# Shifted planes written out to DRAM, first stacks loaded as one transfer each, second stacks filled by ScalarE copies and two late loads

## The chip, the cores and the metric

The kernel runs on one core of one Trainium2 chip. The metric is the device time of one execution in microseconds (us). Engines: TensorE (PE in the profile; PEld is its weight load), VectorE (DVE), ScalarE (ACT), GpSimd (POOL) and SyncE (SP), which here only issues transfers. ACT also issues transfers of its own.

## The reference, cut to what matters

```python
def _gn(v, G=32): ...                  # group norm, 2 channels a group
def _L0_conv_ref(x, weight, scale):    # 3x3 convolution of signs
    y = conv(sign(x), sign(weight), padding=1)
    return y * scale[None, :, None, None]
def _L1_conv_ref(x, ...):              # involution, 7x7, 16 groups of 4 channels
    r = relu(batchnorm(w_r @ x + b_r))             # 64 -> 16 channels
    ker = w_s @ r + b_s                            # 16 -> 49*16: a 7x7 kernel for each pixel and group
    for ki in range(7):
        for kj in range(7):
            out += xp[:, :, :, ki:ki+H, kj:kj+W] * ker[:, :, ki*7+kj][:, :, None]
    return out
x = x + _L0_conv_ref(_gn(x), ...)      # x is (32, 64, 56, 56), float32
x = x + _L1_conv_ref(_gn(x), ...)
```

## The kernel before

Two images make a pair; 16 pairs go through one after the other, and nearly all time is the involution. The kernel swaps its order: for each patch of the normalised image it first multiplies by the weights of every reduced channel (PE), multiplies that by r (DVE, `prod`), and adds up (POOL `folded`, then PE `sums`).

**Strips and units.** The image of a pair is cut into 7 strips of 8 columns (`E = 7`). A strip has 8 units (`GP = 8`), each for two of the 16 groups, so a pair has 56 units, numbered n = 0 to 55. A unit is 8 matmuls of `taps` (L567) into a bank of two halves, one DVE product (L788) and one POOL addition (L361). Three PSUM banks go round among units, convolution chunks (`conv`), transposes (`t`), the reduction (`red`) and outputs, in the order that `turns` lists; a PE step waits until the bank's user of three turns ago has been read.

**Stacks.** The matmuls of strip e read patches from two tiles in SBUF: `X1` ("patches", three buffers, the first stack) and `X2` ("patches2", two buffers, the second stack). A stack's 128 partitions are 8 planes of 16 partitions; a plane is an image part (0 the fp16 value, 1 its fp16 rest) shifted by some rows. On before:
- `first_stack(e)` on SP: eight transfers from DRAM, one a plane (16 partitions, 4 pieces of 3584 B each; L283). It waits until strip e-3 has been read by the matmuls, and that the parts of its pair are in DRAM.
- `second_stack(e)` on SP: two transfers (planes that the first stack hasn't; L291). The other five planes stand in partitions 0 to 95 of the first stack, and ACT copies them there (`copy_high`, L428, four copies of 96 partitions a strip) in the strip before the one that needs them.
- `taps` of a strip's first unit waits for the first stack, for the second stack's transfers, and for the copies.

`PLANES` is the table of part, shift, first partition and partition step of each plane.

**How the parts come to DRAM.** In pair p, while its strips run, pair p+1 is prepared: sums of the image on DVE (n = 0 to 3), `sign` on ACT (n = 5), convolution chunks (n = 11, 12, 14, 17), `root` and `normalize` on ACT (n = 18, 21), four transposes (n = 28, 30, 34, 36), each followed by `high` on ACT (L400) and `low` on DVE (L779), which write the two fp16 parts into a tile with two slots, then `parts_out` on SP (two transfers of 256 KB for each of the four; L266). `high` of transpose k waits until `parts_out` of k-2 has landed. At n = 37 and 38 `red` and `relu` (ACT, L408) make r, and `spread` on SP copies it in 16 transfers of 49 KB (L301) from the tile "blocks" to the tile "relu" that the products read. The first product of the next pair waits for it.

**Results.** `gather(e)` on ACT (L416) takes a strip's sums from PSUM and writes them to DRAM, `rows(e)` on ACT reads them back rearranged, `arrange` on ACT (L450) writes them into "blocks" (the same memory as r before the spread), at n = 46 for strips 0 to 3 and at n = 13 of the next pair for strips 4 to 6; PE transposes them back and DVE adds them to the image, which `store` on SP writes out.

**What sets the order.** Each engine's program is written out by hand, and so is the SP queue: in strip s of pair p it issues the second stack of e+1, the first stack of e+2, `parts_out` 0 and 1 in strip 3, and 2, 3 and the spread in strip 4; the image of pair p+2 is loaded in strip 3. SP works through that list in order, so an entry that waits holds all behind it.

```python
COPY_AT = {0: 0, 1: 1, 4: 2, 5: 3}     # unit of the strip: which of the four copies of the next strip
SUMS_B, BIAS, SUMS_A, ROWS_AT = 3, 6, 7, 7 # units of gather, bias matmuls, first half of sums, rows
```

## Time and profile before

| | before |
|---|---|
| three runs | 1944.62 us median (1939.9 to 1957.48) |
| the profiled execution's own time | 1947.81 us |
| its span, first to last instruction | 1945.9 us |
| granted TensorE clock, mean | 0.922 of full speed |
| PE, DVE, ACT, POOL busy | 83%, 71%, 54%, 52% |
| DMA: moved, mean rate | 410.67 MB, 211 GB/s |
| transfers issued for stacks | 1120 of 224 KB |

The page gives one execution. Times of an instruction are ns or us; "idle before, releaser" is how long its engine had stood still before it and what ended that. In a timeline, "x8" is eight instructions merged in one row. SPq and ACTq are rows of the transfer-issuing sequencers: their time is that of issuing, not of the transfer. Strips are told apart in the timeline by SP's rows: `first_stack(e+2)` starts as soon as strip e-1 has been read.

### The profile page before, as it was taken

The page shows a single profiled execution, that of the slowest core. Times are in us where ns is not written, and L with a number is a line of the kernel's source. Part 1 is how long each engine was busy: PE and PEld are TensorE (multiplying, and loading weights), DVE is VectorE, ACT ScalarE, POOL GpSimd, SP SyncE. Part 2 cuts the span into 40 slices and gives each one's busy share as a digit, 9 for nine tenths or more (in the row PEclk, how much of TensorE's full clock was granted, in tenths as well). Part 3 has the DMA queues.
Part 4 walks back from the last instruction along what each step waited for, and adds up shares of the span by engine and source line. Part 5 has one row for each costly group of instructions (what it writes and reads, how often), then busy time and mean ns, then how long its engine had stood idle before and what let it go on. Part 6 is the DMA issues. An engine that isn't in the chain of part 4 may idle for free.

```text
span 1945.9 us, 38822 instructions
## 1 busy us (share of the span) xinstructions
PE 1615.7 (83%) x15072; PEld 730.2 (38%) x15072; DVE 1377.2 (71%) x1699; ACT 1054.9 (54%) x758; POOL 1016.5 (52%) x904
## 2 busy tenths in 40 slices
PE   3488897979889798897978889798897978889785
PEld 2233443434344343343434344343343433344342
DVE  6476786858678686786858678676786858678574
ACT  2355566555656455565545656454565545656443
POOL 1145565454655555465554655555565454655573
PEclk8699998999999899998989999898998999999897
DMA  3669899797998979799797998979799797988992
GB/s 108 166 168 242 187 261 217 189 245 175 253 211 229 231 192 245 183 260 208 204 229 187 257 199 238 226 188 241 188 254 215 197 236 181 254 206 227 208 248 85
DMA packets 211592, 410.67 MB, mean 211 GB/s; under 512 B 83822, under 2 KB 131231, under 8 KB 207263
## 3 DMA queue, kind: packets, MB, share of 16 engines
q1 hardware_dynamic: 136144, 356.79, 73.1%
q10 hardware_dynamic: 75264, 51.39, 10.2%
q8 instruction: 119, 1.95, 0.5%
q14 instruction: 65, 0.53, 0.1%
HBM read 310.30 MB, written 84.93 MB: 203 GB/s over the span
## 4 chain that ended last, share of the span: by engine, by line
POOL 49%; issue 42%; PE 2%; SPq 2%; DVE 2%; DMA 2%; ACT 1%; POOLq 1%; ACTq 0%; DVEq 0%
POOL folded L361 49%; SPq L301 1%; PE ybank L508 1%; POOLq L360 1%; SPq L283 0%; DMA patches<-parts_dram 0%; PE ybank L567 0%; DMA xs<-x_dram 0%; DVE rowsums L730 0%; DVE prod L788 0%; DMA parts_dram<-parts 0%; PE ybank L537 0%; PE ybank L548 0%; ACT patches L428 0%; ACT sgn L381 0%
## 5 line engine op out<-in xcount | busy, mean ns | idle before, releaser
L361 POOL TENSOR_TENSOR folded<-prod 128x448 f32<-128x448 f32 x896 | 1010.8, 1141 | 911.7 <-DVE prod L788 910.9
L788 DVE TENSOR_TENSOR prod<-ybank,relu 128x896 f32<-128x896 f32 x896 | 960.9, 1088 | 405.7 <-PE ybank L567 336.3
L567 PE MATMUL ybank<-patches,wspan 128*64 128x448 f16 x7168 | 863.2, 383 | 240.8 <-ACT patches L428 106.0
L428 ACT ACTIVATE patches<-patches 96x1792 f16<-96x1792 f16 x448 | 736.6, 1689 | 554.7 <-DMA patches<-parts_dram 273.7
L567 PEld LDWEIGHTS ybank<-patches,wspan 128*64 128x64 f16 x7168 | 400.2, 117 | 757.2 <-issue 421.7
L508 PE MATMUL ybank<-sgn,convw 128*128 128x448 bf16 x1008 | 206.4, 358 | 21.4 <-ACT sgn L381 17.0
L585 PE MATMUL obank<-folded,esum 128*32 128x448 f32 x1792 | 214.8, 551 | 1.5 <-POOL folded L361 1.5
L578 PE MATMUL obank<-patches,wbias 128*32 128x448 f16 x3584 | 197.1, 363 | 0.0
L508 PEld LDWEIGHTS ybank<-sgn,convw 128*128 128x128 bf16 x1008 | 93.7, 98 | 135.3 <-issue 31.5
L578 PEld LDWEIGHTS obank<-patches,wbias 128*32 128x32 f16 x3584 | 87.1, 98 | 103.8 <-issue 50.9
L746 DVE SCALAR_TENSOR_TENSOR xs<-ybank,scale,xs 128x896 f32<-128x896 f32 x64 | 66.0, 1032 | 74.9 <-PE ybank L508 74.8
L779 DVE TENSOR_TENSOR parts<-ybank,parts 128x1024 f16<-128x1024 f32 x64 | 78.3, 1223 | 38.3 <-ACT parts L400 38.0
L400 ACT ACTIVATE parts<-ybank 128x1024 f16<-128x1024 f32 x64 | 65.7, 1027 | 63.1 <-PE ybank L537 59.4
L599 PE MATMUL ybank<-back,blocks 128*128 128x128 f32 (+1 forms) x448 | 61.1, 281 | 43.9 <-DVE prod L788 36.0
L416 ACT ACTIVATE osb<-obank,alpha 128x448 f32<-128x448 f32 x112 | 69.6, 621 | 40.0 <-PE obank L585 39.6
L450 ACT ACTIVATE blocks<-rows 128x1792 f32<-128x1792 f32 (+1 forms) x32 | 54.1, 1691 | 46.3 <-DMA relu<-blocks 33.4
L599 PEld LDWEIGHTS ybank<-back,blocks 128*128 128x128 f32 (+1 forms) x448 | 47.4, 150 | 75.7 <-DVE prod L788 49.5
L750 DVE BATCH_NORM_STATS2 bn<-xs 128x6 f32<-128x448 f32 x112 | 70.3, 627 | 3.9
L537 PE MATMUL ybank<-ident,xn 128*128 128x128 f32 x512 | 71.0, 284 | 1.0 <-DVE parts L779 0.2
L800 DVE TENSOR_TENSOR xs<-ybank,xs 128x1024 f32<-128x1024 f32 (+1 forms) x64 | 61.8, 966 | 12.1 <-PE ybank L599 12.0
L392 ACT ACTIVATE xn<-xs,small 128x1568 f32<-128x1568 f32 x32 | 58.9, 1897 | 17.1 <-DVE small L772 17.0
L730 DVE TENSOR_REDUCE rowsums<-xs 128x14 f32<-128x784 f32 x64 | 61.1, 958 | 9.5 <-DMA xs<-x_dram 9.5
(90 smaller groups left out, 378.0 us busy)
## 6 DMA issues: line engine op xcount, KB each, us to landing
patches<-parts_dram SPq DMA_DIRECT2D x1120, 224.0 KB, 7.1
parts_dram<-parts SPq DMA_DIRECT2D x128, 256.0 KB, 5.4
xs<-x_dram SPq DMA_DIRECT2D x16, 1568.0 KB, 9.7
sums_dram<-osb ACTq DMA_DIRECT2D x112, 224.0 KB, 6.2
rows<-sums_dram ACTq DMA_DIRECT2D x112, 224.0 KB, 6.7
out_dram<-xs SPq DMA_DIRECT2D x16, 1568.0 KB, 5.9
relu<-blocks SPq DMA_DIRECT2D x256, 49.0 KB
patches<-gb_dram SPq DMA_DIRECT2D x1, 784.0 KB
```

Of the source, the lines that this page charges most:

```text
L361: pool.tensor_tensor(folded[:, u % 8, :], prod[:, u % 2, 0, :], prod[:, u % 2, 1, :], ALU.add).then_inc(fold_done, 1)
L416: act.activation(osb[:], Obank[e % 2][:, 0:N], ACT.Copy, scale=alpha[:]).then_inc(o_read, 1)
L428: act.activation(X2[0:COPIED_ROWS, e % 2, at], X1[0:COPIED_ROWS, e % 3, at], ACT.Copy).then_inc(copied, 1)
L508: mm = pe.matmul(bank("conv", p, k)[:, i, 0:CW], convw[:, tap, :], sgn[:, CR * row + dh:CR * row + dh + CR, dw:dw + W], start=(tap == 0), ...
L537: mm = pe.transpose(bank("t", p, k)[:, y, 128 * h:128 * h + 128], xn[:, COLS * cy:COLS * cy + COLS], ident[:])
L567: mm = pe.matmul(bank("unit", p, n)[64 * t:64 * t + 64, h, 0:N], wspan[:, stack, g, h, :], of_group(e, stack, g), start=(stack == 0), stop ...
L578: pe.matmul(Obank[e % 2][32 * t:32 * t + 32, 0:N], wbias[:, stack, g, :], of_group(e, stack, g), start=(stack == 0 and i == 0), stop=False)
L585: mm = pe.matmul(Obank[e % 2][32 * (gp // 2):32 * (gp // 2) + 32, 0:N], esum[:, 16 - 16 * (gp % 2):48 - 16 * (gp % 2)], folded[:, 4 * half ...
L599: mm = pe.transpose(bank("out", p, k)[:, i, rows * n:rows * (n + 1)], V[0:rows, by].rearrange("m b g c -> m (b g c)"), back[0:rows, group, ...
L750: link(dve.bn_stats(bn[:, row, :], at[:, i, :]))
L779: dve.tensor_tensor(at(1), bank("t", p, k)[:], at(0), ALU.subtract).then_inc(low_done, 1)
L788: dve.tensor_tensor(prod[:, u % 2].rearrange("m h (n c) -> m h n c", c=GC), bank("unit", p, n)[:, :, 0:N].rearrange("m h (n c) -> m h n c" ...
```

## The change

`parts_out` now writes all ten planes out, each already shifted, into two DRAM tensors: `D0` holds the eight planes of the first stack side by side, `D1` the two planes that only the second stack has. That is ten transfers for k = 0 and six for each of k = 1, 2, 3 (28 a pair, where there were 8 of 256 KB), of rows of 1024, 768 or 512 B; a source that goes to several planes is read once for each of them in the same transfer. `first_stack` is one transfer of 128 partitions by 4 pieces of 3584 B. Partition 8r+q now holds row r of plane q. The second stack's order is such that six of its eight planes (one of them unused) stand where the first stack has them, so ACT copies all 128 partitions, and planes 3 and 7 are then overwritten by two transfers that ACT itself issues after the four copies. The copies move to units 0 to 3, `rows(e-2)` to unit 3 (it was `rows(e-1)` at 7), `gather` to 4. The spread and the image load move to strip 5, behind the first stack's transfer. r gets a tile of its own (`rsum`), so `relu` and `arrange` lose three waits; `arrange` of the second group moves from n = 13 to 15.

```diff
-PLANES = (((0, 0, 32, 4), (0, 4, 0, 2), (0, 1, 33, 4), (1, 0, 96, 2),
-           (0, 2, 34, 4), (1, 1, 1, 2), (0, 3, 35, 4), (1, 2, 97, 2)), ...
+PLANES = (((0, 0), (0, 2), (0, 4), (1, 1), (0, 1), (0, 3), (1, 0), (1, 2)),
+          ((0, 0), (0, 2), (0, 4), (1, 3), (0, 1), (0, 3), None, (1, 4)))
+LOADED = (3, 7)
-FIRSTLOAD, SECONDLOAD = 16 * 8, 16 * 2
+FIRSTLOAD, SECONDLOAD = 16, 16 * 2
-DWRITE = 16 * 2
+DWRITE = (16 * 10, 16 * 6)
-ARRANGE1_AT, ARRANGE0_AT = 13, 46
-SUMS_B, BIAS, SUMS_A, ROWS_AT = 3, 6, 7, 7
+ARRANGE1_AT, ARRANGE0_AT = 15, 46
+SUMS_B, ROWS_AT, GATHER, BIAS, SUMS_A = 3, 3, 4, 6, 7
-COPY_AT = {0: 0, 1: 1, 4: 2, 5: 3}
+COPY_AT = {0: 0, 1: 1, 2: 2, 3: 3}
...
-        rsum = V[:].rearrange("p y b g c -> p (y b g c)")[:, 0:PX * 2 * HW // POS].rearrange("p (x n) -> p x n", x=PX)
+        rsum = sb("rsum", [128, PX, 2 * HW // POS])
...
 def parts_out(p, k):
-                for l in range(2):
-                    sp.dma_start(D[p % 2, l].rearrange(...)[:, :, k, :], Ev[:, l, k % 2]).then_inc(d_written[k], 16)
+                def run(dram, planes, q, l, y, shift, many):
+                    src = Ev[:, l, k % 2, y]
+                    if k == 0:
+                        for i in range(many):
+                            cut = BLOCK * (shift + i)
+                            sp.dma_start(dram[b, :, q + i, 0:4 * BLOCK - cut], src[:, cut:]).then_inc(d_written[k], 16)
+                        return
+                    dst = bass.AP(..., ap=[[planes * RUN, 128], [RUN - BLOCK, many], [1, 4 * BLOCK]])
+                    sp.dma_start(dst, src.unsqueeze(1).broadcast_to((128, many, 4 * BLOCK))).then_inc(d_written[k], 16)
+                run(D0, Q, 0, 0, 0, 0, 3)
+                run(D0, Q, 4, 0, 1, 0, 2)
+                run(D0, Q, 6, 1, 0, 0, 2)
+                run(D0, Q, 3, 1, 1, 0, 1)
+                run(D1, 2, 0, 1, 1, 1, 1)
+                run(D1, 2, 1, 1, 0, 2, 1)
 def first_stack(e):
-                for l, a, row, step in PLANES[0]:
-                    sp.dma_start(X1[row:row + 15 * step + 1:step, e % 3, :], plane(e, l, a))...
+                sp.dma_start(X1[:, e % 3, :].rearrange("p (j n) -> p j n", j=JX), stack(D0, e)).then_inc(first_in[e % 3], 16)
-            def second_stack(e):    # on SP, waits y_ready
...
                     e = E * p + s
-                    if e + 1 < EALL:
-                        second_stack(e + 1)
...
                         if s == 4:
                             parts_out(p + 1, 2)
                             parts_out(p + 1, 3)
+                        if s == 5:
                             spread(p + 1)
-                    if s == 3 and p + 2 < pairs:
+                    if s == 5 and p + 2 < pairs:
...
-                act.activation(X2[0:COPIED_ROWS, e % 2, at], X1[0:COPIED_ROWS, e % 3, at], ACT.Copy).then_inc(copied, 1)
+                act.activation(X2[:, e % 2, at], X1[:, e % 3, at], ACT.Copy).then_inc(copied, 1)
+            def second_stack(e):    # on ACT
+                act.wait_ge(copied, JX * (e + 1))
+                ...
+                for i, q in enumerate(LOADED):
+                    src = bass.AP(tensor=D1.tensor, ..., ap=[[2 * RUN, 16], [8 * RUN, JX], [1, JY * 128]])
+                    act.dma_start(X2[q:128:Q, e % 2, :]..., src).then_inc(second_in[e % 2], 16)
...
 def arrange(group):
-                act.wait_ge(r_spread, SPREAD * min(p + 1 + (group % 2 == 0), pairs))
...
+                    if n % GP in COPY_AT and e + 1 < EALL:
+                        copy(e + 1, COPY_AT[n % GP])
+                        if COPY_AT[n % GP] == JX - 1:
+                            second_stack(e + 1)
+                    if n % GP == ROWS_AT and e > 1:
+                        rows(e - 2)
+                    if n % GP == GATHER and e > 0:
+                        gather(e - 1)
```

The SP queue in strips 3 to 6 of a pair ("patches" is both stacks' tile, "parts_dram" the DRAM tensor of the parts). Before:

```order
L266 DMA parts_dram<-parts 256x1x512 x4
L254 DMA xs<-x_dram 128x3136
L291 DMA patches<-parts_dram 16x4x1792 x2
L283 DMA patches<-parts_dram 16x4x1792 x8
L266 DMA parts_dram<-parts 256x1x512 x4
L301 DMA relu<-blocks 16x1x784 x16
L291 DMA patches<-parts_dram 16x4x1792 x2
L283 DMA patches<-parts_dram 16x4x1792 x8
```

Now, from the last rows of `parts_out(p+1, 1)` on ("planes_dram" stands for D0 and D1):

```order
L281 DMA planes_dram<-parts 128x512 x3
L302 DMA patches<-planes_dram 128x4x1792
L281 DMA planes_dram<-parts 128x3x512
L281 DMA planes_dram<-parts 128x2x512 x2
L281 DMA planes_dram<-parts 128x512 x3
L281 DMA planes_dram<-parts 128x3x512
L281 DMA planes_dram<-parts 128x2x512 x2
L281 DMA planes_dram<-parts 128x512 x3
L302 DMA patches<-planes_dram 128x4x1792
L311 DMA relu<-rsum 16x1x784 x16
L257 DMA xs<-x_dram 128x3136
L302 DMA patches<-planes_dram 128x4x1792 x4
```

The second stack's rows are gone from SP, ten stack entries a strip have become one, the spread stands behind a first stack and not ahead of one, and the image load stands behind the spread.

ACT in strip 4 (L400 and L408 are `high` and `relu`, L416 with L420 `gather`, L441 `rows`, L428 the copies). Before:

```order
L428 ACTIVATE patches<-patches 96x1792 x2
L400 ACTIVATE parts<-ybank 128x1024
L416 ACTIVATE osb<-obank,alpha 128x448
L420 DMA sums_dram<-osb 128x448
L400 ACTIVATE parts<-ybank 128x1024
L428 ACTIVATE patches<-patches 96x1792
L408 ACTIVATE blocks<-ybank,red_bias,red_scale 128x2x392
L428 ACTIVATE patches<-patches 96x1792
L408 ACTIVATE blocks<-ybank,red_bias,red_scale 128x2x392
L441 DMA rows<-sums_dram 32x16x112
```

Now, the same strip (L434 the copies, L445 the second stack's transfers, L408 `high`, L414 `relu`, L422 and L426 `gather`, L457 `rows`):

```order
L434 ACTIVATE patches<-patches 128x1792 x2
L408 ACTIVATE parts<-ybank 128x1024
L434 ACTIVATE patches<-patches 128x1792 x2
L445 DMA patches<-planes_dram 16x4x1792 x2
L457 DMA rows<-sums_dram 32x16x112
L408 ACTIVATE parts<-ybank 128x1024
L422 ACTIVATE osb<-obank,alpha 128x448
L426 DMA sums_dram<-osb 128x448
L414 ACTIVATE rsum<-ybank,red_bias,red_scale 128x2x392 x2
```

All four copies and the two transfers now stand ahead of the strip's second `high`; both `relu` come after them in one piece.

## Rows read from the trace of the kernel before

**Rows 1.** The page's second part: busy tenths of 40 slices, DMA share, GB/s.

```profile
DMA  3669899797998979799797998979799797988992
DMA packets 211592, 410.67 MB, mean 211 GB/s; under 512 B 83822, under 2 KB 131231, under 8 KB 207263
q1 hardware_dynamic: 136144, 356.79, 73.1%
q10 hardware_dynamic: 75264, 51.39, 10.2%
```

**Rows 2.** Waits: engine, line, what it waited for; us in total, times, longest.

```profile
PE ybank L567 <- ACT patches L428: 106.0, 29, 20.7
PE ybank L567 <- DMA patches<-parts_dram: 103.9, 15, 8.1
ACT patches L428 <- DMA patches<-parts_dram: 273.7, 43, 13.0
SPq L266 <- DVE parts L779: 134.9, 43, 44.7
```

**Rows 3.** Timeline of PE, strip 5 to the next pair's strip 0: start, length.

```profile
981.92 0.95 PE L567 MATMUL ybank<-patches,wspan 128*64 128x448 f16 x8
992.71 0.96 PE L585 MATMUL obank<-folded,esum 128*32 128x448 f32 x8
1001.50 4.60 PE L567 MATMUL ybank<-patches,wspan 128*64 128x448 f16 x24 [7.82 <-DMA patches<-parts_dram]
1014.63 0.96 PE L585 MATMUL obank<-folded,esum 128*32 128x448 f32 x8
1019.49 2.83 PE L567 MATMUL ybank<-patches,wspan 128*64 128x448 f16 x14 [3.90 <-ACT patches L428]
```

**Rows 4.** Timeline of the transfers that SP issues, the same stretch and the next spread.

```profile
963.54 5.73 SPq L266 DMA_DIRECT2D parts_dram<-parts  x4
971.51 5.02 SPq L283 DMA_DIRECT2D patches<-parts_dram  x8
976.63 4.42 SPq L266 DMA_DIRECT2D parts_dram<-parts  x4
983.16 13.50 SPq L301 DMA_DIRECT2D relu<-blocks  x16
996.76 1.26 SPq L291 DMA_DIRECT2D patches<-parts_dram  x2
998.25 5.01 SPq L283 DMA_DIRECT2D patches<-parts_dram  x8
1100.75 12.07 SPq L301 DMA_DIRECT2D relu<-blocks  x16
```

**Rows 5.** Busy time by stretch: bounds; PE, PEld, DVE, ACT, POOL; PEclk, DMA share, GB/s.

```profile
939.00:946.00 7.00, 6.12 (x51) 2.84 (x49) 6.47 (x12) 0.87 (x1) 4.50 (x4) 1.00 1.03 244
951.50:953.50 2.00, 2.00 (x38) 0.85 (x36) 1.86 (x7) 1.12 (x1) 0.06 (x1) 1.00 0.96 401
56.00:65.00 9.00, 3.42 (x32) 0.40 (x32) 2.55 (x3) 4.14 (x4) 0.00 (x0) 0.74 0.69 227
```

**Rows 6.** Timeline of ACT in strips 4 to 6.

```profile
971.67 1.00 ACT L400 ACTIVATE parts<-ybank 128x1024 f16<-128x1024 f32 x1
975.30 1.03 ACT L400 ACTIVATE parts<-ybank 128x1024 f16<-128x1024 f32 x1 [1.24 <-PE ybank L537]
993.08 3.28 ACT L428 ACTIVATE patches<-patches 96x1792 f16<-96x1792 f16 x2 [0.46 <-PE ybank L567]
998.79 1.70 ACT L450 ACTIVATE blocks<-rows 128x1792 f32<-128x1792 f32 x1 [2.43 <-DMA relu<-blocks]
```

**Rows 7.** By line, issue to landing: L283, L291, then L441 (`rows`).

```profile
DMA to landing us min/median/max: 3.0/7.4/15.0
DMA to landing us min/median/max: 3.3/5.5/12.9
DMA to landing us min/median/max: 2.8/6.7/16.7
```

**Rows 8.** Timeline at the start: the first parts and the first product.

```profile
54.53 8.41 SPq L266 DMA_DIRECT2D parts_dram<-parts  x8
85.28 1.09 DVE L788 TENSOR_TENSOR prod<-ybank,relu 128x896 f32<-128x896 f32 x1 [23.56 <-DMA relu<-blocks]
```

More of the change, by code:

```diff
@@ L398, in high @@
                     before = 4 * p + k - 2
-                    act.wait_ge(d_written[before % 4], DWRITE * (before // 4 + 1))
+                    act.wait_ge(d_written[before % 4], DWRITE[before % 4 > 0] * (before // 4 + 1))
                 act.activation(Ev[:, 0, k % 2], bank("t", p, k)[:], ACT.Copy).then_inc(high_done, 1)
@@ L427, in copy_high @@
                 at = slice(COPY * j, COPY * (j + 1))
-                act.activation(X2[0:COPIED_ROWS, e % 2, at], X1[0:COPIED_ROWS, e % 3, at],
-                               ACT.Copy).then_inc(copied, 1)
+                act.activation(X2[:, e % 2, at], X1[:, e % 3, at], ACT.Copy).then_inc(copied, 1)
+            def second_stack(e):
+                act.wait_ge(copied, JX * (e + 1))
+                if e >= 2:
+                    act.wait_ge(second_in[e % 2], SECONDLOAD * (e // 2))
+                p = e // E
+                for i, q in enumerate(LOADED):
+                    src = bass.AP(tensor=D1.tensor, offset=(2 * (128 * (p % 2) + 4 * JX * (e % E)) + i) * RUN,
+                                  ap=[[2 * RUN, 16], [8 * RUN, JX], [1, JY * 128]])
+                    act.dma_start(X2[q:128:Q, e % 2, :].rearrange("p (j n) -> p j n", j=JX), src).then_inc(second_in[e % 2], 16)
             def rows(e):
@@ L473, in _ @@
                         relu(p + 1, RED_AT[n])
-                    if n % GP == SUMS_B and e > 0:
+                    if n % GP in COPY_AT and e + 1 < EALL:
[5 more added lines that the diff above has]
+                    if n % GP == GATHER and e > 0:
                         gather(e - 1)
-                    if n % GP in COPY_AT and e + 1 < EALL:
-                        copy_high(e + 1, COPY_AT[n % GP])
-                    if n % GP == ROWS_AT and e > 0:
-                        rows(e - 1)
                     if more and n == SIGN_AT:
@@ L489, in _ @@
                         arrange(2 * p)
+            rows(EALL - 2)
             gather(EALL - 1)
@@ L850, in constants @@
             for stack in range(2):
-                for part, a, row, step in PLANES[stack]:
+                for q, plane in enumerate(PLANES[stack]):
+                    if plane is None:
+                        continue
+                    part, a = plane
                     sel = stack if part or stack == 0 else 2
@@ L856, in constants @@
                         if 0 <= ky < K and 0 <= kx < K:
-                            c[ky * K + kx, C_SEL + 384 * pos + 128 * sel + row + step * r] = 1
+                            c[ky * K + kx, C_SEL + 384 * pos + 128 * sel + Q * r + q] = 1
     for m in range(128):
```

38 lines of the change are left out of this document (15 added, 23 removed), and 3 rows, old and new, of the table PLANES.

## The prediction

> **What bounds the kernel now.** I read the waits first. Summed over the run, PE stands still before a unit's matmuls for 106.0 us because of ACT's copies and for 103.9 us because of a stack's transfer [rows 2]. The longest single one, 20.7 us, is the start. (106.0 + 103.9 - 20.7)/16 = 11.8 us a pair.
>
> The timeline says where. Strip 5 ends its matmuls at 993.67 us, and strip 6 begins at 1001.50 after 7.82 us of waiting for a transfer; strip 6 ends at 1015.59, and the next pair's strip 0 begins at 1019.49 after 3.90 us of waiting for the copies [rows 3]. So 11.7 us of this pair are two waits, and together with the sum above I take these two as the whole of it. The pair lasts 117.6 us, from one spread to the next [rows 4].
>
> SP's queue explains both. It issues 16 spread transfers in 13.50 us, from 983.16; only then, at 996.76, come the second stack of strip 6 and, at 998.25, the first stack of strip 0 [rows 4]. The matmuls of strip 6 wait for the first, the copies for strip 0 wait for the second.
>
> The transfers themselves are the next bound: queues 1 and 10 together take 83.3% of the 16 DMA engines' span, and most slices stand at 7 to 9 tenths [rows 1]. What to see in the rates: a stretch in which only stacks are loaded is fully busy at 244 GB/s, one in which the image is stored is fully busy at 401 GB/s [rows 5]. A busy DMA engine moves stack planes at 0.6 of the rate it reaches elsewhere. ACT's copies wait 273.7 us for first stacks [rows 2]. POOL, which the page's chain shows most, has half its time idle and follows DVE.
>
> **The change part by part**, for one pair.
>
> *SP's queue.* Stack issues fall from 70 to 7. Eight first-stack issues take 5.02 us and two second-stack ones 1.26 [rows 4], so 44 us a pair go. The spread moves behind the first stack of the next pair's strip 0, and no second stack stands behind it any more. Both waits of [rows 3] lose their cause: minus 11.7 us. `parts_out` goes from 8 issues to 28. Four take 4.42 us with a wait in them, eight at the start 8.41 with waits [rows 4, 8]; without the waits about 0.6 us each; 28 cost 17 us, and SP has the 44.
>
> *The second stack's chain.* What was parallel is now serial: all four copies, then two issues on ACT, then the transfer. Two copies take 3.28 us [rows 6], four 6.6; 128 partitions by 1792 elements should cost ACT what 96 did, since its time went by elements. Two issues add about 0.6. The landing: the same two transfers took 3.3 us at least and 5.5 in the middle [rows 7]. Chain from the end of strip e-1 to the second stack of e+1: 6.6 + 0.6 + 5.5 = 12.7 us, 10.5 at best.
> - Strip 6: the last matmuls of strip 4 end at 982.87, and PE is free for strip 6 at 993.67, 10.8 us later [rows 3]. New wait: 12.7 - 10.8 = 1.9 (0 at best).
> - Strip 0: `arrange` at n = 46 now waits for `rows` of strip 3, which ACT only issues behind strip 6's chain: 982.9 + 6.6 + 0.6 = 990.1, landing 2.8 to 6.7 later [rows 7], arranged after 1.7 [rows 6]: 994.6 to 998.5. Then the chain: 1007.3 to 1011.2. PE would be free for strip 0 at 1015.59 - 7.82 + 1.9 = 1009.7. Wait 0 to 1.5; I take 1.5, because the landings under load have been nearer to the median.
> - Strip 1: its first stack stands behind the spread and behind the 1568 KB of the image, but strip 0 is long. 0.5.
> - Strips 3 and 4: 12 to 14 us for the chain, with `normalize`, `root` and `high` between the copies. 0.5 each.
>
> *ACT's order in strips 3 and 4.* `high` at n = 28 now stands behind all four copies, the second stack's issue and `rows`, not behind two copies: two copies later (3.3 us), of which half is covered by PE's two spare banks: 1.5. `high` at n = 36, which ran at 975.30 [rows 6], likewise: two copies and two issues come first, 1.6. DVE's `low` and all products stand behind it. 3.1 together (1.5 to 5). `high` of k = 2 and 3 also waits for `parts_out` of k = 0 and 1, now 10 and 6 issues (6 and 4 us) where two stood. The first `high` of strip 4 ran at 971.67, 8.1 us after SP began on the first parts at 963.54 [rows 4, 6], so this just fits; at 1 us an issue it would not.
>
> *DMA load.* A pair wrote 8 x 256 KB = 2.1 MB. Now k = 0 writes 128 x (4 x 1024 + 4 x 768 + 2 x 512) B and each other k 128 x 10 x 1024 B, 5.0 MB in all: 2.9 MB more. Such writes ran at 227 GB/s at a share of 0.69, so 329 at full share [rows 5]: 8.8 us more. Against that, 12.8 of the 16 MB of stacks come in transfers of 128 partitions. If these run at the 401 GB/s of the other 128-partition transfer instead of 244 [rows 5], they take 32 us and not 53. Sum: 0.833 x 117 = 97 us, minus 20.6, plus 8.8: 85 us of 114. If they stay at 244: 106 of 114. I take the first, half-heartedly, and charge 0.4 for collisions. The Trainium skill, "SBUF — State Buffer", section "Door 1: The DMA port swizzle", states that partitions reach 16 ports by groups of four, so that 16 partitions at a step of 2, as six of the ten planes have here, reach only 8 of them; "DMA: Bandwidth & Descriptors", section "The descriptor swizzle", gives each engine of a 128-partition transfer one port. The 244 against 401 of the trace agrees. By that rule the stacks run at the faster rate and the two late planes, at a step of 8, at the slower.
>
> *Own tile for r.* `arrange` waited 2.43 us for the spread at 998.79 [rows 6]; that wait goes, and I booked the one that takes its place above. The moved image load waits for nothing that PE needs until the sums of the next pair.
>
> *Ends.* Start: 28 issues instead of 8, from 54.53 on [rows 8], delay the first stack by 6 to 10 us; then copies and second stack in a chain, where now the first product waits for the spread until 85.28 [rows 8]. Plus 9. In the last pair no spread stands in the way before, yet strips wait for stacks; minus 6.
>
> Sum for a pair: 11.7 - (1.9 + 1.5 + 0.5 + 1.0 + 3.1 + 0.4) = 11.7 - 8.4 = 3.3 us gained. 15 x 3.3 = 50; 50 + 6 - 9 = 47. The profiled execution took 1947.81 us, so 1901; it lies 3 above the median of the runs. I say 1900.
>
> **The rivals.**
> 1. *Nothing moves.* The stacks keep 244 GB/s, the queues are busy for 106 of 114 us, and landings on ACT's queue rise by about 1 us. Three to four strips' waits follow, and the 3.3 us are gone: 1935 to 1965, say 1950. For it: the trace has no 128-partition load out of this DRAM layout, so 401 may have to do with the image's layout and not with the partitions. Against it: the surplus is in packets that the queues take well.
> 2. *The chain is the new bound, slower.* Place: copies to second stack, on ACT. If it lands after 7.4 us, as half of the first-stack transfers took or more, and `rows` nearly (6.7) [rows 7], each of strips 6, 0, 1, 3, 4 waits 1.9 us longer: 9 us more a pair, 5.7 worse than before: 1945 + 86 + 3 = 2034. It decides from a landing of about 6.4 us on. For it: the first stack of e+2 is issued at the same moment as the copies begin, and the same engines move both. The Trainium skill, "DMA: Bandwidth & Descriptors", section "Queues, rings and completion order", says an engine goes round between its queues packet by packet, which would double the second stack's moving time while a first stack is under way. Against it: a first stack at 401 GB/s is through in 4.6 us, before the copies end.
> 3. *All hidden.* Landings of 3.3 us, so waits of 0 at strips 6, 0, 1, 3, 4, and 1.5 for ACT's order: 11.7 - 1.9 = 9.8 a pair, 147 + 6 - 9: 1801.
>
> **How the numbers follow.** Chances: forecast 0.43, nothing moves 0.22, slower 0.22, all hidden 0.13. The forecast's own range is 1870 to 1930: chain 1 us shorter or longer changes three or four waits, about 2 us a pair, 30 us. The range of 8 in 10 reaches from 1830 (towards the third rival) to 1990 (halfway into the second). About 1% is what a measurement of this kernel can tell from no change. Faster by over 1% (below 1925): nearly all of the forecast, 0.13 of the third and a little of the first, 0.54. Within 1% (to 1964): 0.22. Slower: 0.24.
>
> **What would show it.** PE's waits of 7.82 and 3.90 us at strips 6 and 0 become 1 to 2 us, and the one at strip 6 names the second stack's transfer on ACT's queue. The first stack lands about 5 to 7 us after its issue, and a stretch with stacks alone shows over 350 GB/s; if it shows 244, rival 1 stands. The second stack's landing, by its line, is 4.5 to 6; over 6.4, rival 2. `high` in strip 4 comes 1.5 us later relative to its transpose; if it instead waits for the parts' transfers, my 0.6 us an issue is wrong, and with it the forecast. The first product comes at 92 to 97 us.

## The result and the profile after

The changed kernel takes 2025.87 us (median of four; 2016.25 to 2028.85) against 1944.18 us (also of four), a ratio of 1.040 with a 95% interval of 1.034 to 1.046: 82 us slower, where 45 us faster was forecast. The profiled execution spans 2021.2 us, 75 us more than the one of before.

The page after, second and third part, against [rows 1]:

```profile
DMA  3738678585875958668585885848768586775873
DMA packets 253316, 456.75 MB, mean 226 GB/s; under 512 B 76398, under 2 KB 172959, under 8 KB 248991
q1 hardware_dynamic: 159952, 351.51, 50.2%
q10 hardware_dynamic: 93184, 102.79, 19.5%
```

The two queues moved 46 MB more in less of the engines' time, 69.7% of the span and not 83.3%. So the transfers did get cheaper, and the time went elsewhere. The waits after, against [rows 2]:

```profile
ACT blocks L465 <- DMA rows<-sums_dram: 204.0, 32, 11.8
PE ybank L586 <- DMA patches<-planes_dram: 146.6, 36, 31.4
DVE parts L798 <- ACT parts L408: 107.4, 52, 5.5
ACT patches L434 <- DMA patches<-planes_dram: 82.7, 16, 13.3
```

ACT waits much less for first stacks (82.7 us, before 273.7) and PE not at all for ACT's copies, but PE waits more for a stack's transfer (it is the second stack), and two waits have grown: `arrange` for the rows (204.0, before 12.9), and `low` on DVE for `high` on ACT (107.4, before 38.0). PE in turn waits for `arrange`, which cost it 7.9 us before:

```profile
PE ybank L618 <- ACT blocks L465: 53.2, 15, 7.7
```

The timeline of PE in strip 6 and at the next strip 0, against [rows 3]:

```profile
1041.88 0.96 PE L604 MATMUL obank<-folded,esum 128*32 128x448 f32 x8
1043.70 2.46 PE L586 MATMUL ybank<-patches,wspan 128*64 128x448 f16 x24 [0.86 <-DMA patches<-planes_dram]
1051.64 1.94 PE L618 MATMUL ybank<-back,blocks 128*128 128x128 f32 x8 [5.48 <-ACT blocks L465]
1062.18 0.96 PE L604 MATMUL obank<-folded,esum 128*32 128x448 f32 x8
1067.05 3.20 PE L586 MATMUL ybank<-patches,wspan 128*64 128x448 f16 x16 [3.91 <-DMA patches<-planes_dram]
```

Strip 6 starts after 0.86 us of waiting, where it was 7.82. But after its third unit PE stands 5.48 us for `arrange`, and strip 0 still starts 3.91 us late. This pair is one of the better ones at strip 6: in the mean over pairs 1 to 14 PE waits 3.33 us at the start of strip 6 and 3.69 at strip 0, both for the second stack's transfers. On the kernel before it was 6.96 and 3.84. ACT in the same stretch, against [rows 6]:

```profile
1032.17 6.45 ACT L434 ACTIVATE patches<-patches 128x1792 f16<-128x1792 f16 x4
1038.65 1.21 ACTq L445 DMA_DIRECT2D patches<-planes_dram  x2
1039.98 0.52 ACTq L457 DMA_DIRECT2D rows<-sums_dram  x1
1040.60 0.63 ACT L422 ACTIVATE osb<-obank,alpha 128x448 f32<-128x448 f32 x1 [1.98 <-issue]
1049.80 1.70 ACT L465 ACTIVATE blocks<-rows 128x1792 f32<-128x1792 f32 x1 [8.57 <-DMA rows<-sums_dram]
1051.40 6.44 ACT L434 ACTIVATE patches<-patches 128x1792 f16<-128x1792 f16 x4
1057.87 1.19 ACTq L445 DMA_DIRECT2D patches<-planes_dram  x2
```

`rows` goes out behind four copies and two issues, lands 9.8 us later, and `arrange` and the copies for strip 0 stand behind it.

The second stack's transfers land after 4.2 us in the median of the whole run, but not where PE waits for them. From the issue of the second transfer to its landing, strips 1 to 4 take 4.0 to 4.4 us in the median (pairs 1 to 14), strip 6 takes 7.7 and strip 0 7.4. Two strips 6 show the difference, first pair 9, then pair 10 (issues of SP and ACT, then the landing of ACT's two):

```profile
1285.47 0.37 SPq L302 DMA_DIRECT2D patches<-planes_dram  x1
1285.80 1.19 ACTq L445 DMA_DIRECT2D patches<-planes_dram  x2
DMA to landing us min/median/max: 7.5/8.1/8.7
```

```profile
1406.74 1.19 ACTq L445 DMA_DIRECT2D patches<-planes_dram  x2
1407.87 0.37 SPq L302 DMA_DIRECT2D patches<-planes_dram  x1
DMA to landing us min/median/max: 3.3/3.7/4.1
```

In pair 9 a first stack is issued just ahead, and PE waits 5.34 us; in pair 10 it is issued 1.1 us after the first of ACT's two transfers, and PE waits 0.73. In the eight strips 6 of pairs 1 to 14 in which the first stack was issued at most 0.2 us after the second transfer, or before it, that transfer took 7.7 to 8.9 us; in the other six, 4.1 to 5.5. No run varied this by itself.

Length of each strip in us, first product to first product, from the timelines of DVE, mean over pairs 1 to 14 of 0 to 15:

| strip | 0 | 1 | 2 | 3 | 4 | 5 | 6 | pair |
|---|---|---|---|---|---|---|---|---|
| before | 13.9 | 21.4 | 17.3 | 12.8 | 15.9 | 17.7 | 17.5 | 116.5 |
| after | 13.8 | 21.3 | 17.4 | 14.6 | 18.6 | 13.7 | 21.8 | 121.4 |

4.9 us a pair, 73 in 15 pairs; the first product comes at 99.27 us and not at 85.28, 14 more; the last pair, from first to last product, takes 82.9 us and not 90.4, 7.5 less. In sum some 80 us, against 75 in the spans (the table's mean leaves pair 0 out).

### The profile page after: what moved, and what is told of

It is laid out like the page before. It is cut to its first block, busy times and chain, and to the rows that moved or that the text cites. A ratio compares the mean times of both kernels' runs of the same rounds, so it can differ in the third digit from the quotient of the medians.

```text
span 2021.2 us, 38357 instructions
## 1 busy us (share of the span) xinstructions
PE 1634.8 (81%) x15072; PEld 729.0 (36%) x15072; DVE 1378.9 (68%) x1699; ACT 1049.6 (52%) x758; POOL 1013.8 (50%) x904
## 3 DMA queue, kind: packets, MB, share of 16 engines
q1 hardware_dynamic: 159952, 351.51, 50.2%
## 4 chain that ended last, share of the span: by engine, by line
POOL 39%; issue 38%; DMA 7%; ACT 5%; DVE 4%; PE 4%; ACTq 1%; SPq 1%; POOLq 0%; DVEq 0%
POOL folded L369 39%; DMA rows<-sums_dram 4%; ACT patches L434 4%; DMA patches<-planes_dram 2%; DVE prod L807 1%; PE ybank L586 1%; ACTq L445 1%; DMA back<-consts_dram 1%; PE ybank L618 1%; ACT blocks L465 1%; DVE parts L798 1%; PE obank L597 1%; PE ybank L567 1%; ACT parts L408 0%; SPq L281 0%
## 5 line engine op out<-in xcount | busy, mean ns | idle before, releaser
L434 ACT ACTIVATE patches<-patches 128x1792 f16<-128x1792 f16 x448 | 725.2, 1684 | 185.1 <-PE ybank L586 97.3
L586 PEld LDWEIGHTS ybank<-patches,wspan 128*64 128x64 f16 x7168 | 390.3, 115 | 742.1 <-issue 350.8
L527 PE MATMUL ybank<-sgn,convw 128*128 128x448 bf16 x1008 | 205.6, 357 | 22.0 <-ACT sgn L389 17.5
L604 PE MATMUL obank<-folded,esum 128*32 128x448 f32 x1792 | 220.2, 564 | 1.5 <-POOL folded L369 1.5
L597 PE MATMUL obank<-patches,wbias 128*32 128x448 f16 x3584 | 206.2, 376 | 0.0
L422 ACT ACTIVATE osb<-obank,alpha 128x448 f32<-128x448 f32 x112 | 70.8, 632 | 180.1 <-issue 146.4
L465 ACT ACTIVATE blocks<-rows 128x1792 f32<-128x1792 f32 (+1 forms) x32 | 54.3, 1697 | 204.0 <-DMA rows<-sums_dram 204.0
L798 DVE TENSOR_TENSOR parts<-ybank,parts 128x1024 f16<-128x1024 f32 x64 | 78.3, 1223 | 107.7 <-ACT parts L408 107.4
L618 PE MATMUL ybank<-back,blocks 128*128 128x128 f32 (+1 forms) x448 | 67.1, 299 | 90.3 <-ACT blocks L465 53.2
L408 ACT ACTIVATE parts<-ybank 128x1024 f16<-128x1024 f32 x64 | 65.5, 1023 | 133.3 <-issue 56.9
L618 PEld LDWEIGHTS ybank<-back,blocks 128*128 128x128 f32 (+1 forms) x448 | 52.3, 161 | 123.7 <-issue 68.0
L389 ACT ACTIVATE sgn<-xs,small 128x3136 bf16<-128x3136 f32 x16 | 46.6, 2914 | 70.4 <-DVE small L758 67.5
L556 PEld LDWEIGHTS ybank<-ident,xn 128*128 128x128 f32 x512 | 57.7, 146 | 52.2 <-DVE parts L798 36.7
```

Source lines behind the costliest of these rows:

```text
L422: act.activation(osb[:], Obank[e % 2][:, 0:N], ACT.Copy, scale=alpha[:]).then_inc(o_read, 1)
L434: act.activation(X2[:, e % 2, at], X1[:, e % 3, at], ACT.Copy).then_inc(copied, 1)
L465: act.activation(V[0:rows].rearrange("m y b g c -> m g y b c"), U[0:rows].rearrange("m g y (b c) -> m g y b c", b=2), ACT.Copy).then_inc(a ...
L527: mm = pe.matmul(bank("conv", p, k)[:, i, 0:CW], convw[:, tap, :], sgn[:, CR * row + dh:CR * row + dh + CR, dw:dw + W], start=(tap == 0), ...
L556: mm = pe.transpose(bank("t", p, k)[:, y, 128 * h:128 * h + 128], xn[:, COLS * cy:COLS * cy + COLS], ident[:])
L586: mm = pe.matmul(bank("unit", p, n)[64 * t:64 * t + 64, h, 0:N], wspan[:, stack, g, h, :], of_group(e, stack, g), start=(stack == 0), stop ...
```

## The experiments

Eighteen runs, each compared with the kernel before on the same chip. "Changed" is the changed kernel, 2026 us.

### Where the time went, first round

**e1: rows where they were.** Edit to the changed kernel:

```diff
-ARRANGE1_AT, ARRANGE0_AT = 15, 46
-SUMS_B, ROWS_AT, GATHER, BIAS, SUMS_A = 3, 3, 4, 6, 7
+ARRANGE1_AT, ARRANGE0_AT = 13, 46
+SUMS_B, ROWS_AT, GATHER, BIAS, SUMS_A = 3, 7, 4, 6, 7
-                    if n % GP == ROWS_AT and e > 1: rows(e - 2)      # behind copy and second_stack
+                    if n % GP == ROWS_AT and e > 0: rows(e - 1)      # behind gather
```

> The changed kernel with one part undone: rows(e-1) at unit 7 again and not rows(e-2) at unit 3 (arrange of the second group at n = 13 again, which the order needs). Theory A (the result transfers): in strip 6 arrange waits about 9 us for rows that ACT issued too late, PE waits about 5.5 us for it before the outputs at n = 50, and the copies for strip 0 start late behind it. Then 4.6 us of strip 6 and 2 to 3 us at strip 0 go, about 7 us a pair, and the time is 1910 to 1935. Theory B (the chain copies, second stack on ACT is the bound, my second rival): what precedes the chain doesn't matter much, the time stays within 15 us of 2026.

Measured: 2035.42 us (ratio to before 1.048, 1.043 to 1.054), no gain. Strip 6 fell from 21.8 to 18.0 us, as theory A has it, and strips 3 and 5 rose from 14.6 and 13.7 to 16.7 and 16.4: ACT now waits for the sums to reach DRAM before it may issue `rows`, and the next strip's copies stand behind that wait.

```profile
ACT patches L434 <- DMA sums_dram<-osb: 98.3, 31, 9.4
```

The wait moved along ACT's queue. That speaks for B, but it doesn't dismiss A: this edit removes one wait and makes another. e13 moves `rows` without that, and gains.

**e2: the spread's new place alone.** Edit to the kernel before: r in a tile of its own (this makes two of the waits needless, not three as said above), and

```diff
                             parts_out(p + 1, 3)
-                            spread(p + 1)
+                        if s == 5:
+                            spread(p + 1)
```

> The kernel before with r in a tile of its own and the spread issued in strip 5, behind the second and first stack of that strip, nothing else. If the two waits of 7.8 and 3.9 us a pair come from the order of SP's queue, as the prediction's first term says, 8 to 11 us a pair go: 1780 to 1830. If they come from the rate of the stack transfers (244 GB/s, queues 83% busy), the stacks land as late as before and it stays at 1920 to 1945.

Measured: 1949.21 us, ratio 1.004 (1.000 to 1.008). Strip 5 fell from 17.7 to 13.6 us, and strips 6, 0 and 1 rose from 17.5, 13.9 and 21.4 to 19.0, 16.4 and 22.8. The waits:

```profile
ACT patches L427 <- DMA patches<-parts_dram: 401.3, 58, 15.1
PE ybank L565 <- ACT patches L427: 139.4, 34, 19.7
```

The copies' wait for first stacks grew from 273.7 to 401.3 us. With SP's order out of the way, the landing of the first stacks was next in line. Whether it is late by the transfers' slow rate alone, this run doesn't tell, for SP now also stands still before those transfers until the parts have landed:

```profile
SPq L281 <- DMA parts_dram<-parts: 102.2, 32, 6.7
```

The first term of my sum, 11.7 us a pair, is worth nothing by itself.

**e3: the copies' new places alone.** Edit to the kernel before:

```diff
-COPY_AT = {0: 0, 1: 1, 4: 2, 5: 3}
+COPY_AT = {0: 0, 1: 1, 2: 2, 3: 3}
```

> The kernel before with its copies at units 0 to 3 and not 0, 1, 4, 5, nothing else. The strips 3 and 4 of the changed kernel are 1.8 and 2.7 us longer than before. If that is ACT's order (high behind four copies), this costs 3 to 4.5 us a pair: 1990 to 2010. If it is the waits of high for the 28 part transfers, or the issue of transfers on ACT, this costs under 1 us a pair: 1945 to 1960.

Measured: 1991.2 us, 46 more than before (1.027, 1.022 to 1.032): 3.1 us a pair. So ACT's order costs this much with no change to any transfer. But only 1.5 of it stands in strips 3 and 4 (13.4 and 16.8 us); strips 0 and 1 grew by 1.9, and PE's wait for the copies at the start of strip 1 from 0.75 to 2.33.

**e4: no second-stack transfers.** Edit to the changed kernel, which leaves out the second stack's two loaded planes after the first strip:

```diff
-                    act.dma_start(X2[q:128:Q, e % 2, :]..., src).then_inc(second_in[e % 2], 16)
+                    if e == 0:
+                        act.dma_start(X2[q:128:Q, e % 2, :]..., src).then_inc(second_in[e % 2], 16)
```

> The changed kernel without the two second-stack transfers (left out but for the first strip, with the waits for them; so two planes of the second stack hold what the copies left and the output is not the reference's). Theory B (the chain's last link bounds): the gaps of 3.2 us at strip 6 and most of 3.8 us at strip 0 go and ACT saves 1.2 us a strip: 6 us or more a pair, 1920 or below. Theory A (arrange bounds strips 6 and 0): 1 to 3 us a pair, 1980 to 2010.

Measured: 1831.43 us, 194 less than the changed kernel. Theory B. The arrange wait fell with it, and `rows` landed after 3.3 us in the median (6.1 in the changed kernel):

```profile
ACT blocks L466 <- DMA rows<-sums_dram: 79.0, 32, 7.9
PE ybank L588 <- DMA patches<-planes_dram: 32.1, 1, 32.1
```

PE's only wait for a stack's transfer is the start's. A pair takes 109.5 us. So 194 us hang on these 224 transfers, as a wait, as traffic, or as ACT's issue time. Strip 6's arrange wait, theory A, hangs on them too; what it costs alone is for e13.

### Partitions of a transfer, and the chain again

**e5: a second stack that needs no copy first**, with planes written out as in the changed kernel; **e6: the same with the chain put back.** e5 gives the six copied planes partitions 0 to 95 and loads the others into 96 to 127:

```diff
+SHARED = ((0, 0, 0, 6), (0, 2, 1, 6), (0, 4, 2, 6), (0, 1, 3, 6), (0, 3, 4, 6))
+PLANES = (SHARED + ((1, 1, 5, 6), (1, 0, 96, 2), (1, 2, 97, 2)), SHARED + ((1, 3, 96, 2), (1, 4, 97, 2)))
-                sp.dma_start(X1[:, e % 3, :]..., stack(D0, e))
+                sp.dma_start(X1[0:96, e % 3, :]..., stack(D0, e, 6))
+                sp.dma_start(X1[96:128, e % 3, :]..., stack(DL, e, 2))
+            def second_stack(e):      # on SP, ahead of first_stack(e + 1); e6: on ACT, behind the copies
+                sp.dma_start(X2[96:128, e % 2, :]..., stack(D1, e, 2)).then_inc(second_in[e % 2], 16)
```

> The changed kernel with another plane order: the six planes that ACT copies stand in partitions 0 to 95, the two that the second stack loads in 96 to 127, so the second stack's transfer (one of 32 partitions, on SP, issued before the first stack of e+2) needs no copy first. First stack as two transfers (96 and 32 partitions), copies at units 0, 1, 4, 5, rows(e-1) at unit 7, image load in strip 3, spread in strip 5; planes written out as in the changed kernel. Theory C (the serial chain copies, then second stack is what the change lost by; written planes and traffic are affordable): PE's waits at the strips' starts shrink to 2 to 4 us a pair, 111 to 114 us a pair, 1850 to 1900. Rival D (the traffic: 46 MB more written, 51 MB of second stacks): the waits stay, 1980 or more.

> The kernel of e5 with the second stack's transfer on ACT behind the four copies, nothing else. Same bytes, same transfers. Theory C: each strip's chain is back and starts at unit 5: 8 us or more a pair over e5, 2000 to 2050. Rival D: within 20 us of e5.

Measured: e5 2082.01 us, e6 2283.6. e5 came out slower than the changed kernel, but that says nothing of the written planes, for its first stacks had become slow. The third part of the page of e5 has

```profile
q1 hardware_dynamic: 177872, 402.90, 78.9%
```

For 51 MB more on this queue (the second stacks) the time rose from 50.2% of 2021 us to 78.9% of 2083. A first stack in 96 and 32 partitions isn't the first stack in 128. As a test of C, e5 is spoiled; e6 against e5 isn't: the same bytes in the same transfers, and the chain behind copies that end at unit 5, with the issue on ACT in place of SP, costs 202 us.

**e7 and e8: the first stack in eight transfers**, out of the changed kernel's DRAM planes, at a step of 8 partitions or in neighbouring ones:

```diff
-                sp.dma_start(X1[:, e % 3, :]..., stack(D0, e)).then_inc(first_in[e % 3], 16)
+                for q in range(Q):                                     # e7
+                    sp.dma_start(X1[q:128:Q, e % 3, :]..., src).then_inc(first_in[e % 3], 16)
+                for i in range(8):                                     # e8
+                    sp.dma_start(X1[16 * i:16 * i + 16, e % 3, :]..., src).then_inc(first_in[e % 3], 16)
```

> The changed kernel with the first stack as eight transfers of 16 partitions at a step of 8, out of the same DRAM planes. If the stacks' slow rate before (244 GB/s alone) came from few partitions a transfer, which reach few of SBUF's ports, a stretch with stacks alone shows 220 to 260 GB/s again; if it came from the layout in DRAM, over 330.

> The same with 16 neighbouring partitions a transfer. If neighbouring partitions share a port in fours, this is as slow as e7 or slower (under 220 GB/s in a stretch with stacks alone); if the DRAM layout decides, over 330.

Measured, one run each: 2206.08 and 2750.86 us. Stretches with stack loads alone, first the changed kernel, then e7, then e8 (bounds; PE, PEld, DVE, ACT, POOL; PEclk, DMA share, GB/s):

```profile
961.50:965.50 4.00, 3.85 (x40) 2.22 (x40) 3.66 (x4) 4.00 (x4) 3.67 (x4) 1.00 1.02 403
```

```profile
1086.00:1090.00 4.00, 4.00 (x40) 1.93 (x38) 3.45 (x5) 4.00 (x4) 3.68 (x4) 1.00 1.06 226
```

```profile
1182.50:1186.50 4.00, 1.96 (x20) 1.06 (x16) 3.72 (x11) 0.64 (x2) 1.13 (x1) 1.00 1.09 125
```

Same source, same pieces of 3584 B, engines fully busy: 403, 226 and 125 GB/s. The layout in DRAM is the same in all three, so it doesn't decide the rate; which partitions one transfer writes does, and with them which of the same pieces it reads. By the port rule of the Trainium skill ("SBUF — State Buffer", "Door 1: The DMA port swizzle"), a transfer of e7 reaches 8 ports and one of e8 only 4 of 16; the measured ratios, 0.56 and 0.31, agree in order and lie somewhat above 8/16 and 4/16.

### The chain's parts, and attempts to mend it

**e9: the second stack's transfers made tiny.** The rest of the two planes is left out.

```diff
-ap=[[2 * RUN, 16], [8 * RUN, JX], [1, JY * 128]]
+ap=[[2 * RUN, 16], [8 * RUN, JX], [1, 64]]
```

> The changed kernel with its second-stack transfers cut to the first 64 of each 1792 elements (the rest of those two planes is left out); the same two transfers on ACT, behind the same four copies, with the same waits. It lies between e4 (no transfer, no wait: 1831) and the changed kernel (2026). Theory C, the serial wait: even a tiny transfer lands 3.3 us or more after its issue, so most of the 195 us stay, 1940 to 2000. Rival D, the traffic of these 16-partition transfers (174 us of the 16 engines' time) and what it delays: 1835 to 1880.

Measured: 1947.02 us. Against e4 (1831) the waits and issues without bytes cost 116 us; the bytes cost the other 79. These transfers land after 2.6 us in the median, the full ones after 4.2:

```profile
patches<-planes_dram ACTq DMA_DIRECT2D x224, 8.0 KB, 2.6
```

```profile
patches<-planes_dram ACTq DMA_DIRECT2D x224, 224.0 KB, 4.2
```

(e9, then the changed kernel). At strips 6 and 0 the tiny ones, too, took 7.1 and 5.8 us.

The strips show where the two parts fall. All that the bytes cost stands in strip 6, 15.8 us here and 21.8 in the changed kernel. The waits at the starts of strips 6 and 0 differ by 0.9 us a pair; what differs most is PE's wait for `arrange`, 11.1 us in all against 53.2, because the rows landed sooner. Of the other part, 3.9 us a pair stand in strips 3 and 4 (13.1 and 16.5 us in e4, 14.7 and 18.8 here), where PE waits for no stack at all: there `high` comes later on ACT, which in e9 stands idle for 60.5 us in all between issuing transfers and `high`, and never in e4. So the 116 us are the serial wait and ACT's issue time together, and no run parts them.

**e10: SP's old order in the changed kernel.**

```diff
-                        if s == 5:
                             spread(p + 1)
-                    if s == 5 and p + 2 < pairs:
+                    if s == 3 and p + 2 < pairs:
```

> The changed kernel with the spread in strip 4 and the image load in strip 3 again, ahead of first stacks, nothing else. If moving them gained what the prediction's first term says, this loses 5 us or more a pair, 2090 to 2140. If, as in e2, their place is worth little, it stays within 20 us of 2026.

Measured: 2086.6 us, 61 more, 4 a pair. Here the new order, of the spread and the image load together, is worth something; in e2, with slow stacks, the spread's place was not. It is a third of what I booked.

**e11, e12: copies on DVE.** Four copies after units 1 and 2, `rows(e-1)` at unit 7; e12 with the image load in strip 3.

```diff
+                    for j in COPY_AT.get(n % GP, ()):      # {1: (0, 1), 2: (2, 3)}, in DVE's queue
+                        copy((UNITS * p + n) // GP + 1, j)  # dve.tensor_copy
```

> The changed kernel with the four copies on DVE (two after unit 1, two after unit 2), the second stack issued by ACT at unit 3, rows(e-1) at unit 7. If the chain and ACT's order are what the change lost by: ACT is free for high and arrange, the chain is 3 to 4 us shorter if DVE copies 16-bit values in under 1 us, PE's waits shrink to 2 to 4 us a pair: 1870 to 1920. If DVE, 68% busy, becomes late itself (copies of 1.9 us each, 53 us a pair), or waits in its queue for first stacks: 2000 or more.

> e11 with the image load in strip 3 again. In e11 the first stack of the next pair's second strip stands behind 1568 KB of image, and DVE's copies wait for it in DVE's own queue. If that matters, 2 to 4 us a pair less than e11; if the image's transfer collides with the parts and first stack of strip 3 as much, the same within 15 us.

Measured: 2189.82 and 2214.77 us. PE's waits at the starts of strips 6 and 0 fell from 7.0 us a pair to 0.7 in e11, so the chain can be hidden, but now PE waits for DVE's products (238.2 us, 34.8 in the changed kernel):

```profile
L815 DVE COPY patches<-patches 128x1792 f16<-128x1792 f16 x448 | 475.7, 1102 | 14.2 <-DMA patches<-planes_dram 14.2
```

448 copies of 1.10 us put DVE at 82% of the span; 423 us more work for 164 us more time. e12 says that the image load's place wasn't it: 25 us slower.

**e13: rows issued ahead of the copies.** Edit to the changed kernel:

```diff
-SUMS_B, ROWS_AT, GATHER, BIAS, SUMS_A = 3, 3, 4, 6, 7
+SUMS_B, ROWS_AT, GATHER, BIAS, SUMS_A = 3, 1, 4, 6, 7
+                    if n % GP == ROWS_AT and e > 1: rows(e - 2)      # ahead of the copy of that unit
```

> The changed kernel with rows(e-2) at unit 1, ahead of the second copy, and not at unit 3 behind all copies and the second stack's issue; nothing else. If arrange's wait in strip 6 (8.6 us for rows, 5.5 us of PE behind it) is a matter of that order, it goes, and the copies for strip 0 start 4 to 6 us sooner: 5 to 7 us a pair, 1920 to 1950. If the wait only moves, as in e1, less than 20 us: over 2005.

Measured: 2000.27 us, 26 less, between the two expectations. PE no longer waits for `arrange` in strip 6 (19.3 us, was 21.8), but its wait at the start of strip 0 grew from 3.7 to 6.1 us, because ACT's copies now wait for first stacks:

```profile
ACT patches L434 <- DMA patches<-planes_dram: 255.5, 33, 13.5
```

against 82.7 us in the changed kernel.

**e14, e15: one or two of the copies on DVE**, on top of e13, with the second stack issued at unit 2:

```diff
-COPY_AT = {0: 0, 1: 1, 2: 2, 3: 3}
+COPY_AT, COPY2_AT = {0: 0, 1: 1, 2: 2}, {1: 3}      # e14: the fourth on DVE after unit 1
+COPY_AT, COPY2_AT = {0: 0, 1: 1}, {1: 2, 2: 3}      # e15: the third and fourth
```

> e13 with the fourth copy on DVE, after unit 1; three stay on ACT. Chain 1.6 us shorter and ACT free earlier, DVE 1.1 us more a strip. If the chain is what bounds the strips' starts: 2 to 4 us a pair less than e13. If DVE's time counts as much (e11), no gain or a loss of up to 4 us a pair.

> e13 with the third and fourth copy on DVE, after units 1 and 2. Chain 3.3 us shorter, DVE 2.2 us more a strip. By the chain alone 4 to 6 us a pair less than e13; by DVE alone (e11: 4 copies cost 10 us a pair over the changed kernel) 5 us more. I expect it within 40 us of e14.

Measured: e14 1938.19 us, 62 less than e13 and even with the kernel before (0.998, 0.996 to 1.000); e15 1944.4, the same. In e14 strips 3, 4 and 5 take 13.1, 16.5 and 10.5 us, but strip 6 takes 22.4.

**e16: tiny planes.** The rest of each written row is left out from the third pair on.

```diff
-                            sp.dma_start(dram[b, :, q + i, 0:4 * BLOCK - cut], src[:, cut:])...
+                            wide = 4 * BLOCK - cut if p < 2 else 32
+                            sp.dma_start(dram[b, :, q + i, 0:wide], src[:, cut:cut + wide])...
```

> The changed kernel with the part transfers of pairs 2 to 15 cut to 32 elements a row (the rest of the planes is left out); same 28 issues, same waits. It takes 5 MB a pair away where the change added 2.9. If written planes matter through high's waits and the queues: 4 us or more a pair less, under 1965. If they are absorbed (the prediction charged 0.4 us a pair): 2000 to 2026.

Measured: 1961.72 us, 64 less than the changed kernel. 14 pairs lose almost all of their 5.0 MB, 4.6 us a pair; for the 2.9 MB that the change added, in proportion 2.7. Strips 3 and 4 stay at 14.8 and 18.6 us, so their growth isn't the part transfers' bytes; strip 6 falls from 21.8 to 16.0. PE's wait for `arrange` falls with it, from 53.2 to 14.9 us in all, and SP's wait for the parts to land before a first stack from 87.5 to 46.1.

**e17, e18: attempts at strips 6 and 0.** e17 is e14 with the image load in strip 6 and, in strip 6 alone, DVE's copy and the second stack's issue at unit 5; e18 is e17 with the transposes and the reduction earlier.

```diff
-                    if s == 5 and p + 2 < pairs:
+                    if s == 6 and p + 2 < pairs:
-                    if n % GP == 2 and e + 1 < EALL:                             # second_stack
+                    if n % GP == (5 if n // GP == 6 else 2) and e + 1 < EALL:
-T_AT, RED_AT = {28: 0, 30: 1, 34: 2, 36: 3}, {37: 0, 38: 1}                       # e18
+T_AT, RED_AT = {26: 0, 28: 1, 30: 2, 32: 3}, {33: 0, 34: 1}
```

> e14 with the image load in strip 6, behind the first stack of the next pair's strip 1, and in strip 6 alone DVE's copy after unit 5 (the second stack's issue there too), so that DVE doesn't wait for a first stack in mid-strip. In e14 that first stack was issued at 1013.3 behind the image and landed at 1027.0. If its place behind the image is what strip 0 waits for: 3 to 5 us a pair less than e14, 1865 to 1895. If the parts' landing (the first stack of strip 0, issued at 1000.0) bounds both: within 15 us of 1938.

> e17 with the four transposes at n = 26, 28, 30, 32 (28, 30, 34, 36 before) and the reduction at 33, 34, so that parts, first stack of the next pair and spread are issued some 6 to 8 us sooner. If the parts' landing bounds the first stack of strip 0: 3 to 5 us a pair less than e17, 1820 to 1850. If the transposes, closer together, wait for the part transfers' two slots instead: as slow as e17 or slower.

Measured: 2001.48 and 1978.03 us, both slower than e14, and neither where any of its expectations had it. In e17 PE waits 13.2 us at the start of strip 0 (mean over the pairs), for the second stack now goes out only at unit 5 of strip 6, which lasts 26.1 us with that wait. e18 takes 8.7 of strip 6 back and gives 3.4 and 3.5 of it to strips 3 and 5: `high` waits for the two part slots,

```profile
ACT parts L411 <- DMA planes_dram<-parts: 112.8, 26, 6.0
```

which the changed kernel shows with 21.8 us. No version that leaves nothing out beat the kernel before by what can be measured.

## Why the prediction was wrong, point by point

- **The two waits removed, 11.7 us a pair: the step that failed.** I took the named releaser's removal for the wait's removal. The order of SP's queue was one of two late things; the first stack's landing was the other (e2: nothing gained). In the changed kernel, where stacks are fast, the order is worth 4 us (e10). There the waits at strips 6 and 0 went from 10.8 us a pair to 7.0, 3.8 less, where the forecast had 11.7 less 3.4 of new waits, 8.3 less. By strips: I had strip 5 (with the wait before strip 6) 5.9 us shorter and strip 6 (with the wait before strip 0) 2.4 shorter; they came out 4.0 shorter and 4.3 longer. That is 8.6 us a pair, about the whole miss of 8.2 (3.3 gained forecast, 4.9 lost). 3.2 of it are PE's new wait for `arrange`, below.
- **The chain, 4.9 us a pair.** The mechanism was right, the size not: without its bytes it costs 116 us over e4, 7.7 a pair, ACT's issues included. I took one landing of 5.5 us for all strips. It was 4.0 to 4.4 in strips 1 to 4, where PE hardly waits for it, and 7.7 and 7.4 in strips 6 and 0, where PE does: 3.3 and 3.7 us of waiting, where I took 1.9 and 1.5. I also put two issues at 0.6 us, though the two in [rows 4] take 1.26; they took 1.2. The waits of 0.5 us each that I booked for strips 1, 3 and 4 came to 0.1 in all. e6, where the same chain starts two units later, shows how steeply it counts.
- **Rows and `arrange`: a missing term.** I moved `rows` behind the chain and followed it to the copies, not to PE, whose outputs at n = 50 wait for `arrange`. I also took a landing of 2.8 to 6.7 us; it was 9.8 in the stretch shown. Strip 6 grew by 4.3 us. PE's waits for `arrange` cost 53.2 us in all, 7.9 before. Undone in a way that keeps the rest (e13), it gives 26 us, since part of the wait moves to strip 0.
- **ACT's order, 3.1 us a pair: the number right, partly by luck.** e3 measures 3.1 on the kernel before, but only 1.5 of it in strips 3 and 4, where I had all of it. In the changed kernel these two grew by 4.5, inside my 1.5 to 5; in e4, with the same order and no second-stack transfers, by 0.9. So most of the growth hangs on the second stack's issue on ACT and not on the copies ahead of `high`.
- **Written planes, 0.4 us a pair: mis-sized.** e16 gives 2.7 for the added bytes, an estimate in proportion. I had the engines' time right (69.7% of a pair of 121 us is 85 us) and left out what waits meanwhile: SP stands 87.5 us before first stacks until the parts have landed (46.1 in e16), and the rows land later (PE's wait for `arrange`, 53.2 us against 14.9). How the 64 us of e16 divide between the two is open.
- **Faster stacks: right.** 403 GB/s where I took 401; with 226 GB/s in its place the changed kernel is 180 us worse (e7, one run).
- **`parts_out` at 0.6 us an issue: about right.** `high` waits 21.8 us in all for part transfers, the whole run.
- **Ends.** The first product came at 99.27 us, 14 later, where I had plus 9. The last pair gained 7.5 us, I had 6.
- **The rivals.** The second, at 2034 us, has the number and the place, the serial chain on ACT. Its condition, a landing of over 6.4 us, isn't met by the line's median (4.2, the sign that I had named) but is met in strips 6 and 0, in 20 of 29 cases, and most often while a first stack is under way, as it said. It asked for that in five strips and got it in two where PE waits; there the waits exceed the forecast by 3.6 us a pair, not 9. The rest of its number is `arrange`, ACT's issues and the start, so that it comes so near is luck. What the runs leave open is how the rest divides: the effects don't add up, since each strip's wait is the later of several. The range ended at 1990 and missed by 36 us.

## What to carry to other kernels

A wait that the profile names has a second-latest cause behind it; before booking its removal, look up when the next input would have come, for every wait of the sum. Turning work that ran side by side into a chain costs wherever its last link lands late, here in two of seven strips, and everything issued behind the chain on the same engine, small transfers too, has to be followed to whoever waits for it. A median landing over the whole run can hide the few that matter (4.2 us here, against 7.7 and 7.4 where PE waits): read landings at the waits. In this kernel a stack is best loaded over all 128 partitions at once: with eight transfers of 16 in its place the changed kernel is 180 us slower (e7).

## What the runs showed of the hardware that I had not expected

- The same 1.8 MB load out of the same DRAM planes, with fully busy engines: 403 GB/s as one transfer of 128 partitions, 226 as eight of 16 at a step of 8, 125 as eight of 16 neighbours. I had expected the direction, not a factor of 3.
- 96 and 32 partitions instead of 128 (e5) brought the load back to about the old rate: queue 1 took 78.9% of the span for 402.90 MB, so 402.90 MB in 0.789 x 2083 us, 245 GB/s. By the same sum it is 251 before and 346 in the changed kernel. The run doesn't tell the 96 from the 32.
- In strips 6 of the changed kernel a 224 KB load on ACT's queue landed after 7.7 to 8.9 us when a 1792 KB load on SP's queue was issued with or before it, and after 4.1 to 5.5 when that came at least 0.6 us later. Even 8 KB took 7.1 us there in the median (e9), against 2.3 in strips 1 to 3.
- Issuing isn't free for ACT: two transfers of the second stack and the one of `rows` kept it idle for 1.98 us before its next instruction (1040.60 in the rows of ACT above).
- DVE copied 128 x 1792 16-bit values in 1.10 us, ACT in 1.68.
